# Reciprocals of the softmax row sums: taken before the transposition instead of after it, with ScalarE emptying PSUM

## The reference

```
x  = layernorm_L0(x + softmax(q k^T / 8 + side, masked) v  @ w_o)      # 16 heads of 64, keys from ctx
x  = layernorm_1 (x + mha(x, x,   sa_*, pair mask))                    # 16 heads of 32, self attention
x  = layernorm_2 (x + mha(x, ctx, ca_*, no mask))                      # 16 heads of 32, cross attention
x  = layernorm_3 (x + relu(x @ ff_w1.T + b1) @ ff_w2.T + b2)
```

## Time and profile before

| | |
|---|---|
| time, median of 3 runs (lowest to highest) | 3939.6 us (3938.47 to 3941.65) |
| profiled execution, its own time | 3942.07 us |
| its span in the trace | 3940.3 us |
| mean granted TensorE clock | 0.993 |
| busy PE, DVE, ACT, POOL | 94%, 70%, 55%, 48% |
| instructions | 63021 |

### The profile page before, as it was taken

The page is one execution under the profiler, slowest core; times in us unless marked ns, Lnnn a source line. Parts: engine busy times, 40 slices in busy tenths (PEclk is TensorE's granted clock), DMA queues, the critical chain, the costliest instruction groups (busy, mean ns, idle before and its releaser), DMA issues.

```text
span 3940.3 us, 63021 instructions
## 1 busy us (share of the span) xinstructions
PE 3715.4 (94%) x20204; PEld 2739.5 (70%) x20204; DVE 2763.4 (70%) x5754; ACT 2166.6 (55%) x4724; POOL 1895.6 (48%) x1853
## 2 busy tenths in 40 slices
PE   8999999999999998999999998999999989999999
PEld 6666766666666666666666666666666658888887
DVE  6666666577777778888888887888888864344434
ACT  5555555555544546777777766777777752111111
POOL 5444444334434334777777665666666632112101
PEclk9999999999999999999999999999999999999999
DMA  6777777555555567666677547776667693112210
GB/s 196 203 214 220 211 204 203 150 154 150 141 143 145 142 194 186 181 178 176 174 177 184 152 141 204 176 178 169 165 165 177 179 229 99 57 59 78 64 34 33
DMA packets 893543, 618.98 MB, mean 157 GB/s; under 512 B 649504, under 2 KB 700192, under 8 KB 892192
## 3 DMA queue, kind: packets, MB, share of 16 engines
q1 hardware_dynamic: 879248, 573.00, 55.1%
q10 hardware_dynamic: 13968, 41.95, 3.3%
HBM read 222.84 MB, written 238.29 MB: 117 GB/s over the span
## 4 chain that ended last, share of the span: by engine, by line
PE 36%; DVE 7%; ACT 6%; issue 6%; DMA 4%; POOL 3%; SPq 1%; DVEq 0%; ACTq 0%; POOLq 0%
PE psV L1613 5%; PE psT L1585 4%; PE psS L1564 3%; PE psS L1509 3%; PE psS L1510 3%; PE psS L1511 3%; POOL QS L2444 3%; PE psJ L1509 2%; PE psJ L1510 2%; PE psJ L1511 2%; PE psT L1509 2%; PE psT L1511 2%; PE psT L1510 2%; ACT PR L1886 2%; DMA OG<-r_rows 2%
## 5 line engine op out<-in xcount | busy, mean ns | idle before, releaser
L2444 POOL TENSOR_SCALAR QS<-QK 32x1024 fp32r<-32x1024 f32 (+2 forms) x1152 | 1242.4, 1078 | 1059.0 <-DVE QK L2106 607.7
L1886 ACT ACTIVATE PR<-PR,MN 128x512 f32<-128x512 f32 x1536 | 1100.8, 718 | 801.8 <-DVE MN L2088 664.1
L2088 DVE CUSTOM_DVE_ANT_0 PR<-psS,RAW 128x512 f32<-128x512 f32 x1024 | 692.8, 682 | 401.5 <-PE psS L1561 324.7
L1585 PE MATMUL psT<-ID,PR 128*128 128x128 f32 x3912 | 598.1, 275 | 61.4 <-ACT PR L1886 59.3
L1585 PEld LDWEIGHTS psT<-ID,PR 128*128 128x128 f32 x3912 | 470.3, 141 | 215.8 <-ACT PR L1886 115.8
L1613 PE MATMUL psV<-plain 128*32 128x512 f32 (+1 forms) x3072 | 509.5, 611 | 21.4 <-DMA plain<-split_rows 10.4
L1564 PE MATMUL psS<-QS 128*128 128x512 f32 x1024 | 456.7, 448 | 59.7 <-DVE PR L2092 33.1
L2092 DVE TENSOR_SCALAR_CACHE_REDUCE PR<-psS 128x512 f32<-128x512 f32 x512 | 344.0, 681 | 82.7 <-PE psS L1564 78.4
L1927 ACT ACTIVATE PR<-psS,COLS 128x512 f32<-128x512 f32 x128 | 88.3, 690 | 563.4 <-PE psS L1511 563.3
L2186 DVE COPY plain<-psT 128x512 f32<-128x512 f32 x530 | 360.3, 680 | 0.0
L1905 ACT ACTIVATE plain<-psT 128x512 f32<-128x512 f32 x448 | 263.6, 589 | 119.1 <-PE psT L1585 115.3
(11 more groups left out here) (163 smaller groups left out, 8253.6 us busy)
## 6 DMA issues: line engine op xcount, KB each, us to landing
split_rows<-plain SPq DMA_DIRECT2D x366, 256.0 KB, 2.8
split_rows<-RAW SPq DMA_DIRECT2D x192, 256.0 KB, 2.7
x<-Y SPq DMA_DIRECT2D x96, 256.0 KB, 2.8
RAW<-x SPq DMA_DIRECT2D x96, 256.0 KB, 3.6
Y<-x SPq DMA_DIRECT2D x96, 256.0 KB, 3.7
kept_c<-R SPq DMA_DIRECT2D x32, 512.0 KB, 3.9
OG<-r_rows SPq DMA_DIRECT2D x128, 128.0 KB, 3.0
kept<-ROWS SPq DMA_DIRECT2D x32, 512.0 KB, 3.8
```

Source lines behind the costliest of these rows:

```text
L1585: mm = nc.tensor.transpose(dst[:, kt * P:(kt + 1) * P], prob(st, k)[:, kt * P:(kt + 1) * P], ID[:, :])
L1886: nc.scalar.activation(prob(st, k), prob(st, k), ACT.Exp, bias=MN[:, k % 8:k % 8 + 1], scale=-1.0, accum_out=row_sums(st, g)[:, qt, j:j + ...
L2088: nc.vector.tensor_tensor_reduce(out=prob(st, k), in0=psS[:, n % 2], in1=FB[:, k % NT], scale=-st.scale, scalar=BIG, op0=ALU.add, op1=ALU. ...
L2444: nc.gpsimd.tensor_scalar(to, pair, 1.0, 1.0, ALU.mult, ALU.mult).then_inc(stacked, 1)
```

## The change

VectorE now takes the reciprocals where the sums lie, in `SM`: 128 partitions of 8 or 16 numbers, written to a new buffer `RS` of which the unused columns are zero. TensorE transposes `RS` instead of `SM` and waits for VectorE's new semaphore `recip_done` instead of for the exponentials. A new step R_COPY lets ScalarE copy the turned rows out of PSUM to `RT`; SyncE's store and TensorE's reuse of the slot wait for that copy (`p_copied`).

In the tables RECIP moves ahead of R_TURN, and R_COPY takes the slot that RECIP had. The key in `in_order` now also keeps the parts of a projection job in sequence, which leaves the order of this kernel's jobs as it was: apart from RECIP and R_COPY the common list is the same, and TensorE, GpSimd and SyncE have the same instructions in the same order (TensorE with `RS` for `SM`).

```diff
@@ STEPS
     "SCALE",
+    "R_COPY",
     "P_HI",
@@ WIDE
+    "RECIP": 4.5,
     "R_TURN": 5,
-    "RECIP": 5.5,
+    "R_COPY": 5.5,
@@ SECOND, and THIRD alike
+    "RECIP": 5,
     "R_TURN": 5.5,
-    "RECIP": 6,
+    "R_COPY": 6,
@@ buffers
-        SM = sb("SM", [P, 2, P])
+        SM = sb("SM", [P, 2, 4 * NT])
+        RS = sb("RS", [P, 2, P])
@@ tensor
             def turn_reciprocals(st, g, b):
-                pe.wait_ge(exp_done, exp_at[st.name, b, st.per_group * NT * (g + 1) - 1])
+                pe.wait_ge(recip_done, recip_at[st.name, b, g])
                 dst = turn_place(st, b, ("R", g))
-                nc.tensor.transpose(dst[:, 0:P], SM[:, g % 2], ID[:, :]).then_inc(t_full, 1)
+                nc.tensor.transpose(dst[:, 0:P], RS[:, g % 2], ID[:, :]).then_inc(t_full, 1)
@@ scalar
+            def copy_reciprocals(st, g, b):
+                act.wait_ge(t_full, turned_at[st.name, b, ("R", g)])
+                act.wait_ge(r_stored, 16 * (group_at[st.name, b, g] - 1))
+                rows = st.per_group * NT
+                nc.scalar.activation(RT[0:rows, :], turned((st.name, b, ("R", g)))[0:rows, 0:P], ACT.Copy).then_inc(p_copied, 1)
@@ vector
             def row_reciprocals(st, g, b):
-                dve.wait_ge(t_full, turned_at[st.name, b, ("R", g)])
-                dve.wait_ge(r_stored, 16 * (group_at[st.name, b, g] - 1))
-                rows = st.per_group * NT
-                nc.vector.reciprocal(RT[0:rows, :], turned((st.name, b, ("R", g)))[0:rows, 0:P]).then_inc(t_evac, 1)
+                dve.wait_ge(exp_done, exp_at[st.name, b, st.per_group * NT * (g + 1) - 1])
+                nc.vector.reciprocal(row_sums(st, RS, g), row_sums(st, SM, g)).then_inc(recip_done, 1)
```

More of the change, by code:

```diff
@@ L407, in timetable @@
                 add(NT * h + table["PV"][kt], "PV", (g, kt))
-            for step in ("R_TURN", "RECIP", "R_STORE", "R_LOAD", "SCALE", "GROUP_HI", "GROUP_LO"):
+            for step in ("RECIP", "R_TURN", "R_COPY", "R_STORE", "R_LOAD", "SCALE", "GROUP_HI", "GROUP_LO"):
                 after = table[step]
@@ L509, in in_order @@
     name = lambda e: (e[1], e[2], e[3].name if e[3] else None, e[4])
-    return [e[1:] for e in sorted(ev, key=lambda e: (own.get(name(e), e[0]), STEPS.index(e[1]), e[4]))]
+    key = lambda e: (e[1], e[2], e[3].name if e[3] else None, e[4], e[5])
+    at = {key(e): own.get(name(e), e[0]) for e in ev}
+    for e in sorted((e for e in ev if e[1] == "JOB" and e[2][1]), key=lambda e: e[2][1]):
+        at[key(e)] = max(at[key(e)], at.get((e[1], (e[2][0], e[2][1] - 1), *key(e)[2:]), at[key(e)]))
+    return [e[1:] for e in sorted(ev, key=lambda e: (at[key(e)], STEPS.index(e[1]), e[4]))]
 OPENING = {
@@ L926, in build @@
         exp_done = sem("exp_done")
+        recip_done = sem("recip_done")
         r_stored = sem("r_stored")
@@ L1040, in before, with row_sums @@
             return NT * (b - 1) + tt
-        def row_sums(st, g):
-            return SM[:, g % 2, 0:st.per_group * NT].rearrange("p (j t) -> p t j", t=NT)
+        def row_sums(st, t, g):
+            return t[:, g % 2, 0:st.per_group * NT].rearrange("p (j t) -> p t j", t=NT)
         def bias_col(st, which, g):
@@ L1105, in build @@
         turned_at, evacuated, exp_at, sent_at, product_at = {}, {}, {}, {}, {}
-        parts_loaded, group_at = {}, {}
+        parts_loaded, group_at, recip_at = {}, {}, {}
         done = {t_evac: 0, p_copied: 0}
@@ L1121, in count_turns @@
                     turned_at[st.name, b, k if step == "TURN" else ("R", k)] = len(turned_at) + 1
-                elif step == "RECIP" or step == "P_LO" and not by_act(st, k):
+                elif step == "P_LO" and not by_act(st, k):
                     done[t_evac] += 1
-                    evacuated[st.name, b, k if step == "P_LO" else ("R", k)] = t_evac, done[t_evac]
+                    evacuated[st.name, b, k] = t_evac, done[t_evac]
                 elif step == "R_LOAD":
@@ L1127, in count_turns @@
                     group_at[st.name, b, k] = len(parts_loaded)
-                elif step == "P_HI" and by_act(st, k):
+                elif step == "R_COPY" or step == "P_HI" and by_act(st, k):
                     done[p_copied] += 1
-                    evacuated[st.name, b, k] = p_copied, done[p_copied]
+                    evacuated[st.name, b, k if step == "P_HI" else ("R", k)] = p_copied, done[p_copied]
+                elif step == "RECIP":
+                    recip_at[st.name, b, k] = len(recip_at) + 1
         passes(count_turns, lambda st: None)
@@ L1886, in exponential @@
                 nc.scalar.activation(prob(st, k), prob(st, k), ACT.Exp, bias=MN[:, k % 8:k % 8 + 1], scale=-1.0,
-                                     accum_out=row_sums(st, g)[:, qt, j:j + 1]).then_inc(exp_done, 1)
+                                     accum_out=row_sums(st, SM, g)[:, qt, j:j + 1]).then_inc(exp_done, 1)
             def split_prob(st, k, b):
@@ L1965, in run @@
                         take(*k)
+                    elif step == "R_COPY":
+                        copy_reciprocals(st, k, batch + off if at is None else at)
                     elif step == "GROUP_HI":
@@ L2017, in _ @@
             nc.vector.memset(COLS[:, NCOL:NCOL + NG], 0.0).then_inc(const_ready, 1)
-            nc.vector.memset(SM[:, :], 0.0).then_inc(const_ready, 1)
+            nc.vector.memset(RS[:, :], 0.0).then_inc(const_ready, 1)
             dve.sem_inc(s_evac, 2)
```

## The result

| | before | after |
|---|---|---|
| time, median (lowest to highest) | 3939.1 us (3938.5 to 3941.7) | 3903.2 us (3901.7 to 3907.6) |
| profiled execution, its own time | 3942.1 us | 3907.6 us |
| its span | 3940.3 us | 3905.8 us |

The ratio is 0.991 (95% interval 0.9892 to 0.9927): 36 us are won, where the prediction had 12.7. Run again beside the experiments, the changed kernel took 3898.5 us, ratio 0.9896 (0.988 to 0.9912).

What follows compares the result with a forecast made beforehand. TensorE, busy 3715 of 3940 us, was the bound: only its idle time counts. L0 +6.3, second groups -7.2, third groups -6.0 and -2.8, load chain -3 sum to -12.7 us, giving median 3927 us, range 3896 to 3948.

Steps and rivals of the forecast that it cites:

- the forecast's own case: Whole kernel: the prediction's main estimate of 3927 us, with its own range 3917 to 3935 us and chance 0.47.
- the first rival: SA and CA: VectorE bounds them throughout, 0.74 us returns in each of 64 groups, -41 us, 3898 us; chance 0.20.
- three signs of being wrong: Small reciprocals over 0.3 us, EXP behind the copy costing TensorE over 0.2 us, or later SA/CA gaps growing by early gains.
- The new reciprocals: VectorE's small SBUF reciprocals ahead of R_TURN: 0.14 us each in L0a and L0b, 0.20 us in SA and CA.
- The rival of a reciprocal that does not shrink: L0a and L0b: each of 45 waits grows by the reciprocal's full length; at 0.50 us, +12 us, 3952 us; chance 0.16.
- 45 waits in L0 grow by 0.14 us, +6.3 us: L0a and L0b: reciprocals ahead of GROUP_LO and the tile copy lengthen each R_TURN wait by 0.14 us, +6.3 us.
- ScalarE's copy: Copy of turned rows from PSUM: 0.30 us each, 38 us of ScalarE in all, mostly into idle time; next EXP queues behind.
- The pessimistic end, 4.4 us: ScalarE's copy at 0.59 us puts another 0.29 us into the 15 second groups, 4.4 us.
- The second groups, 15 x 0.48 = -7.2 us: SA and CA second groups: the score behind R_TURN starts 0.48 us sooner, 15 times, -7.2 us.
- The third groups, -6.0 and -2.8 us: Third groups: scores sooner by 0.86 us in 7 of SA (-6.0 us), 0.40 us in 7 of CA (-2.8 us).
- The load chain, -3 us: SA and CA: SCALE's wait for reciprocals from DRAM shrinks, about 10 waits at 0.3 us, -3 us, ends 0 and 8 us.
- First and fourth groups, counted at nothing: SA and CA: no gain outside the 29 of 64 groups with score waits; elsewhere TensorE has work of its own.

## Why the prediction was right in sign and short in size

It said faster, through VectorE in SA and CA, at a small price in L0. That held. The time was 24 us below the predicted one: inside the stated range, but outside the 3917 to 3935 us of the forecast's own case and nearest to the first rival. None of its three signs of being wrong came. By its steps:

**The new reciprocals.** Taken at 0.14 and 0.20 us. The records say 0.20 and 0.25 us, but the next instruction starts 0.116 and 0.160 us after the reciprocal's start (medians of 64 each), and that is what the queue pays. The old instruction, and the long one of the experiments, starts its successor after 0.87 us. Between 16 and 128 numbers this is (0.865 - 0.160) / 112 = 0.0063 us a number; the prediction's 0.0074 was an upper bound. The rival of a reciprocal that does not shrink fell with the first row.
On the disputed start-up of the Trainium skill, "VectorE: DVE Perf Modes", "The TRN2 errata": its 58 cycles (0.06 us) are what the start-to-start times leave when 0.0063 us a number is taken off (0.066 and 0.059 us), its 150 cycles (0.16 us) are what the records' lengths leave (0.150 and 0.145 us). Both figures hold here, for different questions.

**45 waits in L0 grow by 0.14 us, +6.3 us.** The listed waits grew by 3.1 us, and the change in L0 alone costs nothing (-6 to +1 us). Three things were off. An instruction costs its start-to-start time, 0.116 us. The place is exposed in the third and fourth groups, not in all that list a wait (the second groups' 16 waits do not grow with the long reciprocals): about 28 of 45. And GROUP_LO behind it shrinks by part of what is put ahead. That the place is a costly one was right: the same instruction at its old length costs 35 us there, as its rule 45 x 0.75 = 34 us says, though only 21 us of it stand in the waits it named.

**ScalarE's copy.** 0.30 us forecast, 0.26 us in the records and 0.17 us start to start. The stall of the transposition behind it was to be 0.20 us in 15 groups; it is 0.07, and moving the copy away wins nothing. The pessimistic end, 4.4 us, had no ground.

**The second groups, 15 x 0.48 = -7.2 us.** This is the mis-sized term. At the very place of the sum the score came 0.80 us earlier: 0.13 us from the smaller stall, and 0.19 us because the score starts 0.42 us behind the transposition's start, while the sum let it wait for the end of the transposition's record, 0.61 us. In CA the distance across that group shrinks by 1.40 us. There the first score gives 0.80 us and the lead grows to 1.38 us by the second. All 29 waits that the prediction counted behind R_TURN, in second and third groups, are gone. In SA and CA together the second distances sum to -13.4 us in the first profiled execution and -10.2 in the second, against the -7.2 us.

**The third groups, -6.0 and -2.8 us**, hold at most in their sum. SA's third distances are mixed and sum to -0.6 us in one execution and -3.3 in the other; CA's sum to -5.4 and -7.2 us, where 0.7 to 1.5 us come back in most batches instead of its 0.4.

**The load chain, -3 us.** 0.3 us were counted where GROUP_LO, and SCALE and the score with it, moved by 0.74 to 0.86 us. SCALE stands 4.6 us behind GROUP_LO (4.75 before) and waits nearly the same time in both (1.62 and 1.53 us): the loads take 3.3 us from the first issue to the last landing in both, and only their start moves.

**First and fourth groups, counted at nothing.** CA's fourth gives 0.50 us and its first 0.22 us in each inner batch, SA's first 0.48. In CA's fourth a score wait of 0.17 us does stand 2.78 us behind R_TURN; the prediction put it at nothing. In SA's first a transposition waits 0.31 us for an exponential 6.83 us behind R_TURN, further than the prediction looked, and in CA's first the product with the values waits 0.16 us for a tile copy. All three waits are gone. CA's fourth needs both the end of VectorE's wait for R_TURN and the short reciprocals; the first groups' shares come for the most part with either alone (0.51 and 0.40 us in SA, 0.22 and 0.15 us in CA with the short ones in the old place and with the long ones in the new place).

**The rival "VectorE is the bound of all of SA and CA"** gave 3898 us, and the two readings are 3903 and 3899. Its sum came close, its reason only in part: it priced the saved length, 0.74 us in each of 64 groups. The experiments divide the win otherwise. The short length alone gives 20 us, the new place with the old length 24 us, both 36 to 38 us, so they overlap by some 7 us (long reciprocals in SA and CA only; the short ones stood in L0 too, where the change alone was worth about nothing). Handing the PSUM copy of 0.2 us, and with it the wait for R_TURN, to ScalarE is worth 11 to 16 us of it, with the reciprocals at the same place and length. In a stage where VectorE is the bound everywhere, 64 x 0.71 us saved would have returned 45 us by the length alone; it returned 20 (16 to 28), and 29 us by the distances of SA and CA in its profiled execution, the shortest of its four. In the changed kernel a part of what VectorE saves goes into the 23 us of longer SPLIT copies. The uncoupling of the two halves of a group, which was held against this rival, was wrong too: GROUP_LO, SPLIT and SCALE hand the lead on.

What stays open: the 6 to 7 us that the edges of L0b give back. With long reciprocals in L0 1.9 us at its start and 3.4 us at its end remain, so most of it is not the length; with short ones in the old place 2.1 us of the end are there as well. What stretches GROUP_LO, and SPLIT in SA and CA. And whether the two halves help each other. No run separates these.

## What to carry to other kernels

Price a small instruction by the distance to the start of the next one on its engine, and a score or a transposition behind another likewise; here the length in the record is about 0.1 us (reciprocals) or 0.2 us (transpositions) longer. Moving a short step to another engine can be worth about as much here as shortening it was (11 to 16 us against 20), where the step has to wait for another engine's result. When a wait is removed, follow the whole period up to the next one of the same place before counting the gain: a lead is handed on through queues in order, and groups without a wait near the edit can gain as well.

## What the runs showed of the hardware

The reciprocal's time goes by the numbers of a partition alone: 0.94 us for 128 of them on 8, 16 or 128 partitions, out of PSUM or SBUF, and 0.24 to 0.25 us for 16 of them from either. A two-operand VectorE instruction of 512 numbers (GROUP_LO) took 0.81 to 0.97 us in one and the same place, with something else ahead of it each time. Single executions of one kernel differ by 11 us (3893 to 3904 us for the changed one), so that moves worth 3 us cannot be told apart. A part of it lies in L0a, where the distances of three kernels with the changed kernel's order there summed to +5.4 to +6.0 us, and those of the changed kernel to +2.7. VectorE's SPLIT copy of 1024 16-bit numbers a partition took 0.87 us in the mean in SA and 0.86 in CA before, 0.97 and 0.96 after, with the same instructions around it but for the reciprocals.
